# Where the second layer norm of the first three batches runs: VectorE in one head group, or GpSimd in two

## The reference

```
h = layernorm(x) * (1 + ca) + sa
x = x + ga * attention(h)            # 16 heads of 16, top-1 feature per head, top-64 keys per query, causal
h = layernorm(x) * (1 + cb) + sb     # the second norm
x = x + gb * experts(h)              # router over 8 experts, each takes its 512 best tokens, two layers
```

## Time and profile before

| | us |
|---|---|
| timed runs | 1014.6, 1017.11, 1017.33, median 1017.11 |
| profiled execution | 1014.52 |
| its span, first to last instruction | 1012.8 |
| TensorE busy | 840.4 (83%) |
| VectorE busy | 654.3 (65%) |
| ScalarE busy | 455.3 (45%) |
| POOL busy | 316.4 (31%) |
| the 16 head groups | from 67.9 to about 672 |

### The profile page before, as it was taken

The page is one execution under the profiler, slowest core; times in us unless marked ns, Lnnn a source line. Parts: engine busy times, 40 slices in busy tenths (PEclk is TensorE's granted clock), DMA queues, the critical chain, the costliest instruction groups (busy, mean ns, idle before and its releaser), DMA issues. The chain is left out here.

```text
span 1012.8 us, 16388 instructions
## 1 busy us (share of the span) xinstructions
PE 840.4 (83%) x6080; PEld 460.6 (45%) x6080; DVE 654.3 (65%) x1504; ACT 455.3 (45%) x572; POOL 316.4 (31%) x466
## 2 busy tenths in 40 slices
PE   6766999988999979989978978883018999999996
PEld 5542444434444434434434534342014777666664
DVE  6858687678687787696794795544876644544441
ACT  2435667765567746466666567640002111222210
POOL 3612433511533512244332212100005343343222
PEclk9868999999999999999999999996557999999998
DMA  4000000000200001200002102001902443442111
GB/s 146 22 1 1 22 22 1 2 1 2 63 22 1 1 26 60 64 1 1 2 1 86 42 1 86 1 22 68 372 23 65 116 101 65 118 115 32 22 21 21
DMA packets 34852, 46.53 MB, mean 46 GB/s; under 512 B 2184, under 2 KB 30928, under 8 KB 34640
## 3 DMA queue, kind: packets, MB, share of 16 engines
q1 hardware_dynamic: 28624, 36.89, 10.9%
q0 software_dynamic: 6144, 8.52, 5.1%
HBM read 32.69 MB, written 12.72 MB: 45 GB/s over the span
## 5 line engine op out<-in xcount | busy, mean ns | idle before, releaser
L927 ACT ACTIVATE p_buf<-ps 128x1024 f32<-128x1024 f32 x288 | 279.3, 1022 | 168.6 <-PE ps L408 150.8
L768 POOL TENSOR_SCALAR_AFFINE_SELECT p_buf<-p_buf 128x512 f32<-128x512 f32 x128 | 95.7, 772 | 321.1 <-ACT p_buf L927 235.4
L436 PE MATMUL ps<-p_buf,vv 128*17 128x512 f32 (+3 forms) x1664 | 152.3, 467 | 14.4 <-POOL p_buf L768 11.7
L408 PE MATMUL ps<-qx,kd 32*128 32x512 f32 (+3 forms) x1280 | 133.2, 508 | 32.9 <-ACT p_buf L927 13.2
L2089 ACT ACTIVATE h_t<-ps,b_t 128x512 f32<-128x512 f32 x64 | 44.0, 687 | 236.4 <-PE ps L2029 236.4
L1261 DVE SCALAR_TENSOR_TENSOR p_buf<-ps,p_buf 128x1024 f32<-128x1024 f32 x64 | 78.3, 1223 | 91.4 <-PE ps L430 44.5
L2039 PE MATMUL ps<-w_sb,h_t 128*128 128x256 f32 x512 | 112.5, 380 | 0.8 <-ACT h_t L2089 0.8
L2029 PE MATMUL ps<-tok_t,w_sb 128*128 128x512 f32 x256 | 112.6, 598 | 0.0
L2039 PEld LDWEIGHTS ps<-w_sb,h_t 128*128 128x128 f32 x512 | 96.6, 190 | 15.3 <-ACT h_t L2089 1.6
L408 PEld LDWEIGHTS ps<-qx,kd 32*128 32x128 f32 x1280 | 56.2, 187 | 98.3 <-issue 93.7
L352 PE MATMUL ps<-w_t,h_t 128*128 128x512 f32 (+1 forms) x224 | 78.4, 494 | 8.0 <-ACT p_buf L927 4.1
(11 more groups left out here) (288 smaller groups left out, 1241.5 us busy)
## 6 DMA issues: line engine op xcount, KB each, us to landing
w_sb<-in_L_ffn_w_dram SPq DMA_DIRECT2D x16, 1024.0 KB, 8.6
h_table<-xr SPq DMA_DIRECT2D x3, 1056.0 KB, 4.6
x_in<-in_L_attn_x_dram SPq DMA_DIRECT2D x6, 512.0 KB, 4.0
out_dram<-xr SPq DMA_DIRECT2D x3, 1024.0 KB, 5.2
xr<-in_L_attn_x_dram SPq DMA_DIRECT2D x3, 1024.0 KB, 5.7
h_table<-xr SPq DMA_DIRECT2D x2, 528.0 KB, 3.2
xr<-in_L_attn_x_dram SPq DMA_DIRECT2D x2, 512.0 KB, 5.3
p_buf<-in_L_wmod_dram SPq DMA_DIRECT2D x1, 1024.0 KB, 8.7
```

The costliest lines, as they stand in the source:

```text
L408: m = pe.matmul(o, key, qx[r, par, t0:t0 + w], start=True, stop=not run)
L436: m = pe.matmul(ps[32 * h:32 * h + HD + 1, 6, o:o + w], vv[:, (gi // NG) % 2, i, HG * (gi % NG) + h, :], p_of(gi, u)[:, h, lo:lo + w], sta ...
L768: m = pool.affine_select(p, p, [[0, HG], [1, P]], ALU.is_ge, 0.0, base=0, channel_multiplier=-1)
L927: act.activation(p_of(gi, u)[:, 2 * a:2 * a + 2, :], buf(w), ACT.Exp, scale=0.25).then_inc(free_of(w)[0], 1)
```

## The change

The second norm of the batches 0 to 2 goes from VectorE to POOL, in four pairs of tiles. For each pair POOL does (x - mean) * rstd tile by tile (two tensor_scalar of 256 columns), then one product with 1 + cb and one sum with sb over both tiles (two tensor_tensor of 512 columns), with a drain ahead of each of these. The pairs (0, 1) and (2, 3) run in the group ahead of `norm_group`, behind `keep` of the second tile and `tri(gi, 3)`; the pair (4, 5) runs in `norm_group` between `tri(gi, 1)` and `tri(gi, 2)`, and the pair (6, 7) between `tri(gi, 2)` and `tri(gi, 3)`. `norm_group` of batch 2 goes from g = 1 to g = 2, so that its transposes, logits and shares go from group 13 to group 14; for the batches 0 and 1 they stay in 7 and 11. The new pairs thus run in the groups 6 and 7, 10 and 11, 13 and 14. VectorE drains after `take_mod` and signals f_bc, for which POOL waits.

```diff
--- before.py
+++ after.py
@@ -206,8 +206,8 @@
...
-        f_otok, f_x2, f_woga, f_h2, f_hev, f_lm, f_lexp, f_lt = (sem(n) for n in (
-            "f_otok", "f_x2", "f_woga", "f_h2", "f_hev", "f_lm", "f_lexp", "f_lt"))
+        f_otok, f_x2, f_woga, f_h2, f_hev, f_lm, f_lexp, f_lt, f_bc = (sem(n) for n in (
+            "f_otok", "f_x2", "f_woga", "f_h2", "f_hev", "f_lm", "f_lexp", "f_lt", "f_bc"))
...
@@ -254,7 +254,7 @@
 
         def norm_group(b):
 
-            return 1 if b == LAST - 1 else 3
+            return 2 if b == LAST - 1 else 3
 
         def halves(b):
 
@@ -769,6 +769,19 @@
                         lo += w
                     m.then_inc(f_tri, 1)
 
+                def second_norm(b, t):
+                    if t == 0:
+                        pool.wait_ge(f_out, 16 * (b + 1))
+                        pool.wait_ge(f_bc, b + 1)
+                    if t % 2 == 0:
+                        h2 = xr[:, t:t + 2, 0:D]
+                        for i in (t, t + 1):
+                            pool.tensor_scalar(xr[:, i, 0:D], xr[:, i, 0:D], mv2[:, i, 0:1], rstd2[:, i:i + 1], ALU.subtract, ALU.mult)
+                        pool.drain()
+                        pool.tensor_tensor(h2, h2, bc[:, D:2 * D].unsqueeze(1).to_broadcast([P, 2, D]), ALU.mult)
+                        pool.drain()
+                        pool.tensor_tensor(h2, h2, bc[:, 0:D].unsqueeze(1).to_broadcast([P, 2, D]), ALU.add).then_inc(f_h2, 2)
+
                 def keep(b, t):
                     pool.wait_ge(f_one, NT * b + t + 1)
                     pool.wait_ge(*free_of(("Y", b, t)))
@@ -849,12 +862,19 @@
                         first_rstd(b + 1, 0)
                     if tiles:
                         keep(b + 1, t0)
+                    if post and g == norm_group(b - 1):
+                        second_norm(b - 1, 4)
                     tri(gi, 2)
+                    if post and g == norm_group(b - 1):
+                        second_norm(b - 1, 6)
                     tri(gi, 3)
                     if g == 0 or g == 3 and pre:
                         stage(gi + 2)
                     if tiles:
                         keep(b + 1, t0 + 1)
+                    if post and g == norm_group(b - 1) - 1:
+                        second_norm(b - 1, 0)
+                        second_norm(b - 1, 2)
                     if g == 1 and pre:
                         first_rstd(b + 1, 1)
                     if tiles:
@@ -1286,6 +1306,7 @@
                 def take_mod(b):
                     m_full(("BC", b))
                     dve.tensor_copy(bc[:, :], ps[:, 7, :]).then_inc(f_mfree, 1)
+                    dve.drain().then_inc(f_bc, 1)
 
                 def residual(b, half):
                     u = ("P", b, half)
@@ -1321,19 +1342,6 @@
                     for t in range(4 * half, 4 * half + 4):
                         dve.scalar_tensor_tensor(xr[:, t, 0:D], x_in[:, t % 4, :], rstd2[:, t:t + 1], bc[:, 0:D],
                                                  ALU.mult, ALU.add).then_inc(f_h2, 1)
-
-                def second_norm(b, half):
-                    if half == 0:
-                        dve.wait_ge(f_rstd2, b + 1)
-                        dve.wait_ge(f_out, 16 * (b + 1))
-                    ts = range(4 * half, 4 * half + 4)
-                    for t in ts:
-                        h = xr[:, t, 0:D]
-                        dve.scalar_tensor_tensor(h, h, mv2[:, t, 0:1], bc[:, D:2 * D], ALU.subtract, ALU.mult)
-                    dve.drain()
-                    for t in ts:
-                        h = xr[:, t, 0:D]
-                        dve.scalar_tensor_tensor(h, h, rstd2[:, t:t + 1], bc[:, 0:D], ALU.mult, ALU.add).then_inc(f_h2, 1)
 
                 def router_max(b, hs):
                     m_full(("LT", b, hs))
@@ -1425,8 +1433,6 @@
                         one_feature(b + 1, t0)
                     if g == 0 and pre:
                         norm_stats(b + 1, 0)
-                    if post and g == norm_group(b - 1):
-                        second_norm(b - 1, 0)
                     if gi:
                         out_rows_of(gi - 1, 1)
                     if g == 0 and post:
@@ -1439,8 +1445,6 @@
                         normalize(b + 1, 0)
                     if tiles:
                         one_feature(b + 1, t0 + 1)
-                    if post and g == norm_group(b - 1):
-                        second_norm(b - 1, 1)
                     if g == 1 and pre:
                         norm_stats(b + 1, 1)
                     mask(gi, 1, 0)
```

## The result

The change makes the kernel slower: 1035.63 us (median of four, 1032.6 to 1036.57) against 1017.22 (1014.6 to 1018.53), ratio 1.0176 [1.0156, 1.0196]. The forecast was 1027, in a range of 1011 to 1036. The profiled execution took 1036.57 us, the longest of the four, and that of before 1014.52, shorter than any of its timed runs; so the profiles lie 22 us apart and the medians 18.4.

The account below looks back on a forecast made before the run. TensorE bounds plain groups, VectorE's instruction order the three norm groups. 2 x (-1.0 + 3.4) + 3.0 = +7.8, with clock +11.3, on the profiled 1014.5 gives 1025.8; plus 1.3 for timed runs: 1027 us, range 1011 to 1036.

Parts of the forecast that it names:

- The rival "faster": POOL idle enough: pv(2) waits 1.8 not 4.0 us, VectorE's delay 1.3 not 3.3; about 1011 us, chance 0.2.
- "the same": One of the two prices, pv(2) wait or VectorE delay, falls away; 1014 to 1018 us, chance 0.2.
- rival (c): Much slower: tensor_scalar 0.67 us, VectorE 5 us late in 6, 10, 13, six low-clock stretches on the path; 1041, chance 0.1.
- signs of being wrong: Select ends before the scan, POOL's pair under 3 us, its tensor_scalar over 0.7, or group 6 under 41 us.
- signs of being right: Include pv(2) waits some 4 us, mask(1,1) wait over 3, group 7 near 37, 14 at 36 to 37, six low-clock groups.
- a pair on POOL: Two tensor_scalar at 0.35, two products at 1.16, two drains at 0.2: 3.4 us, 4.1 at the dear end.
- The timetable: Group 7: second product slips in before VectorE's scan, selects follow, pv(2) at about 354.8; TensorE waits 4.0 us.
- no second wait: Group 7: pair (6,7) and tri(3) run to 359.2, pv(3) is reached at 359.7, so TensorE does not wait there.
- Contention: POOL's pairs take turns with VectorE's keys: +3.4 us each in groups 6 and 10; group 13's mask 3.2 later.
- Clock: Six stretches at 1.2 GHz instead of three, each up to 1.7 us, 10 in all; 3.5 us taken.
- The move to group 14: Batch 2's row store and the last residual's load leave a group later on SP's queue; costed at nothing.
- +7.8 without clock: Sum over the touched groups: 2 x (-1.0 + 3.4) for 7, 6, 11, 10, plus 3.0 for 13 and 14.

## Why the prediction was right, and where it was not

**Direction and mechanism.** Slower, by two new waits, as forecast: pv(2) for a POOL select in 7, 11 and 14, and the matmul behind `mask(1,1)` in 6, 10 and 13. The rival "faster" named its own test: pv(2) in group 7 before 353, which is 359.2 with the group 6.2 us later; it came at 362.12. The rivals "the same" and "faster" needed one of the two prices to fall away; neither did.

**What was luck.** The time lies 0.4 us inside the range, two of the four runs lie above it, and it is outside the 1020 to 1033 that the prediction gives its own forecast. It is nearer to rival (c), 1041, than to 1027, and of (c)'s conditions the dear tensor_scalar came, and dearer still; that VectorE would be late by 5 us didn't. One of the prediction's own signs of being wrong came true: a tensor_scalar over 0.7 us. Others of its signs of being right failed: 7 took 40.0 instead of 37, 14 took 39.9 instead of 36 to 37, and the wait behind `mask(1,1)` stayed under 3 us. For 7 and 11 even the sign was wrong, +1.9 instead of -1.0. So the account of which waits come is right, and a price in it is badly off.

**The term that was mis-sized: a pair on POOL.** I took 0.35 us for a tensor_scalar, as half a select, and 0.67 as the dear end; it takes 1.22, outside both. The select has one input and one operation; half its time was no bound for an instruction with two per-partition operands and two operations, and no row of before had one; the other estimate there, 0.38, fails the same way. The pair is 5.3 instead of 3.4 us. The three groups were 2.9, 2.9 and 3.4 us over their forecast, 9.2 in all. Two runs enclose what the price is worth there: 1.4 us off each pair (one product) gave 4.9 us back, and 2.6 off (no tensor_scalar) gave 9.9. The error of 1.9 lies between, by a straight line some 6 to 7 us; that is an estimate, as the 9.9 also holds some clock (group 14, which lost its low-clock stretch, gained 4.5 and the others 3.0 and 2.4).

**The timetable.** For group 7 I had pv(2) at 354.8, that is 361.0 after the shift of 6.2; it came at 362.12. The scan hid part of the dearer pair, since the second product had to wait for it anyway. The longer pair showed one step on, which the forecast had closed with "no second wait": `tri(3)` ended at 367.89 instead of 365.4, and pv(3) began at 368.73 instead of 365.9. No wait shows ahead of it, as TensorE came there at the lower level; at the upper one, in the run with five idle products, it waited 1.39 us. So the wait at pv(2) alone (5.09 against 4.0) understates the miss, and 2.5 of group 7's 2.9 us are the late `tri(3)`.

**Contention.** Forecast +3.4 for 6 and 10; without low clock group 6 takes 42.0 in two experiments, +2.5, and group 10 of the run with five idle products 42.3, +2.4. The turns didn't fall as I dealt them. I had charged n_lo and kb for the tensor_scalars' turns; kb kept its 0.28 us, and n_lo was held 1.1 us by the first pair's first product. k_opp is 1.08 us longer, as forecast (1.1), but by the second product and not the third, so that agreement is luck; the second pair's products began only at 332.29, 0.6 us ahead of the mask, and mx, k_far and k_max, charged 1.8 us together, lost under 0.3. For group 13 the mask came 1.3 us later and not 3.2. I looked only at the keys there, but POOL's last two products run until 621.36, beside the queries, and TensorE waits another 2.01 us for z_rank. That the group then took 32.8, near the 31.7 forecast, is luck: in the run with half on POOL the wait is absent and it took 30.7.

**Clock.** Six groups with the lower level, as forecast. Taken was 3.5 us; measured are 2.7 in group 6 and 1.3 in group 10 (43.6 against 42.3), and about 2 in 7, 11 and 14 together: 6, and group 13 isn't separated. The sign of the argument was right and the place wrong in part: where TensorE has no slack (6 and 10), a stretch of 3.4 us costs 1.3 to 1.6 us (group 6 took 43.5 with one such stretch and no tensor_scalars), near the full 1.7; in 7, 11 and 14, where POOL's queue bounds, twice as much low clock is nearly free.

**The move to group 14.** Costed at nothing in itself, and the run that does it alone agrees.

**The balance.** Over the forecast's +7.8 without clock lie 9.2 us in 7, 11 and 14, 2.1 in 6 and 10 and 1.1 in 13, 12.4 together, of which the 3.5 taken for the clock covers a part: 8.9 us short by the profiles, 8.6 by the medians. By the estimate above 6 to 7 of the 12.4 come from one price, the largest part; more clock than was taken, and less contention than was charged, make up the rest, and group 13 isn't separated. The actual time lies at the upper end of the range for that reason.

**Open.** Why a wait is followed by one or two low-clock stretches, or by none: group 6 had waits of 2.67 to 2.76 us in six kernels and showed none in two, one in two, two in two. Groups that the change doesn't touch show more of them too in the changed kernel: 12 takes 41.5 us against 40.0, and all of them together 2.9 us more. And no run moved the early pairs in 6, 10 and 13, so whether their contention can be avoided on POOL isn't known.

## What to carry to other kernels

An idle engine's queue is not idle capacity: ask which instruction behind the new work releases the bottleneck, and put the work behind that one; the same pairs one place later cost 11 us less here. Work on POOL that reads two tensors is paid for by VectorE's two-input passes as well, so a norm moved there should stand where VectorE has slack, or stay on VectorE at an earlier place. Price an instruction that the trace has never shown by a wide bracket, and let its dear end be that of the most complex neighbour, with two operations counted as two (here 2 x 0.67 = 1.34, which would have held 1.22).

## What the runs showed of the hardware

- A POOL tensor_scalar with two per-partition scalars takes 1.22 us for 256 columns, nearly as much as a two-tensor product of 512 (1.27). With a per-tile scalar spread as the second operand, a product of 512 columns takes 1.04.
- Beside VectorE's keys a tensor_scalar is itself stretched (up to 2.37 us) but doesn't hold VectorE up: k_opp, begun 0.76 us after a tensor_scalar, kept its 0.68 us. Products do hold it, n_lo at 1.25 us (0.15 in an undisturbed group) and k_opp at 1.76. Fills, which read nothing, made VectorE's second mask 0.5 us late where reading pairs made it 1.3 late.
- With the same starts to 0.01 us, VectorE's `uq` and a POOL product took turns one way in the changed kernel (2.30 and 1.42 us) and the other way with half of the norm on POOL (1.22 and 2.69).
- Five idle products in a wait of 5 us kept the granted clock at 1.00 in three groups, and this bought 2 us, because TensorE wasn't the bound there.
